# A four-layer graph network kernel: the add of beta moved from VectorE to GpSimd in the node tail, and two VectorE steps taken ahead of the scaling by gamma

## The reference, cut to what matters

```
h = relu(layernorm(x)); x = x + GAT(h)          # attention layer, two convolutions
h = relu(layernorm(x)); x = x + LightGCN(h)     # three hops of weighted sums over edges
h = relu(layernorm(x)); x = x + L2(h)           # messages and node updates
h = relu(layernorm(x)); x = x + GCN(h)          # three layers with weights conv_w
```

```
h2 = relu(layernorm(x))
update = relu(h2 @ Wu1a + bu1) @ Wu2 + bu2
x3 = x + layernorm(h2 + update) * gamma + beta
h3 = relu(layernorm(x3))
x0 = relu(h3 @ fc1 + fc1_b), then three products by conv weights with relu, then out = x3 + (...) @ fc2 + fc2_b
```

## Time and profile before

| | |
|---|---|
| median of 3 runs | 6715.88 us (6671.08 to 6734.13) |
| profiled execution, span from first to last instruction | 6034.3 us |
| the phase, 2381 to 3549 us of the span | 1168 us |
| VectorE busy in the phase | 1036.25 us |
| ScalarE busy | 773.95 us |
| PE busy | 841.98 us |
| GpSimd busy | 593.38 us |

### The profile page before, as it was taken

The page is one execution under the profiler, slowest core; times in us unless marked ns, Lnnn a source line. Parts: engine busy times, 40 slices in busy tenths (PEclk is TensorE's granted clock), DMA queues, the critical chain, the costliest instruction groups (busy, mean ns, idle before and its releaser), DMA issues. The chain is left out here.

```text
span 6034.3 us, 73632 instructions
## 1 busy us (share of the span) xinstructions
PE 3347.4 (55%) x17186; PEld 2352.5 (39%) x17363; DVE 4133.5 (68%) x14902; ACT 2890.5 (48%) x6936; POOL 3733.6 (62%) x3700
## 2 busy tenths in 40 slices
PE   0534777737330000777777758888688854454443
PEld 0423554627320000444444436666466644343322
DVE  7359999639491995998989967777377755454332
ACT  0954777313100222666666647777477743232110
POOL 0664776767675576645536546665577627676776
PEclk9767999767665555899999989999899976566666
DMA  2223665637321664434435445554244447564333
GB/s 67 80 93 119 199 200 189 191 91 192 84 51 43 163 186 124 121 109 110 116 100 121 110 128 186 189 188 158 84 151 150 141 143 246 175 200 145 119 123 100
DMA packets 512359, 827.25 MB, mean 137 GB/s; under 512 B 108999, under 2 KB 193843, under 8 KB 510796
## 3 DMA queue, kind: packets, MB, share of 16 engines
q1 hardware_dynamic: 396011, 629.55, 32.2%
q0 software_dynamic: 115936, 193.21, 14.3%
HBM read 382.25 MB, written 452.03 MB: 138 GB/s over the span
## 5 line engine op out<-in xcount | busy, mean ns | idle before, releaser
L3074 POOL DMA_INDIRECT gcn_ring<-GT,gcn_index x588 | 586.6, 998 | 199.1 <-issue 170.1
L3175 DVE SCALAR_TENSOR_TENSOR gcn_acc<-gcn_acc,cont,gcn_ring 128x128 f32<-128x128 f32 x588 | 203.6, 346 | 562.5 <-DMA gcn_ring<-GT,gcn_index 561.4
L1602 POOL DMA_INDIRECT light_ring<-C,light_s_u x392 | 390.5, 996 | 285.9 <-DVE light_acc L1645 178.7
L482 POOL DMA_INDIRECT J<-packed,sort_place x392 | 423.7, 1081 | 155.2 <-issue 120.5
L3257 PE MATMUL gcn_psA<-ident,gcn_h 128*128 128x128 f32 x588 | 154.9, 415 | 598.5 <-DVE gcn_h L3178 598.0
L3224 ACT ACTIVATE gcn_hT<-gcn_psA 128x512 f32<-128x512 f32 x147 | 87.8, 597 | 698.0 <-PE gcn_psA L3257 697.5
L3257 PEld LDWEIGHTS gcn_psA<-ident,gcn_h 128*128 128x128 f32 x588 | 100.1, 207 | 636.9 <-DVE gcn_h L3178 636.9
L1447 ACT ACTIVATE tail_h<-tail_x,tail_nmr,tail_std 128x128 f32<-128x128 f32 x784 | 320.8, 484 | 9.2 <-DVE tail_nmr L1377 9.2
L2321 POOL DMA_INDIRECT out<-source_x,source_own_u x196 | 193.7, 988 | 208.8 <-DVE source_x L2407 163.1
L473 POOL DMA_INDIRECT got_s<-TAB,src_u x196 | 202.1, 1031 | 123.7 <-issue 63.0
L1496 PE MATMUL tail_psT<-ident,tail_h 128*128 128x128 f32 x784 | 128.9, 289 | 266.3 <-ACT tail_h L1447 266.3
(11 more groups left out here) (637 smaller groups left out, 12801.6 us busy)
## 6 DMA issues: line engine op xcount, KB each, us to landing
T<-front_t SPq DMA_DIRECT2D x196, 272.0 KB, 2.1
C<-light_acc SPq DMA_DIRECT2D x147, 256.0 KB, 2.1
source_c<-C SPq DMA_DIRECT2D x147, 256.0 KB, 4.9
GT<-source_r SPq DMA_DIRECT2D x147, 256.0 KB, 2.1
gcn_own<-GT SPq DMA_DIRECT2D x147, 256.0 KB, 3.5
RC<-gcn_own SPq DMA_DIRECT2D x147, 256.0 KB, 3.6
RG<-gat_rows SPq DMA_DIRECT2D x98, 264.0 KB, 3.9
front_x<-in_x SPq DMA_DIRECT2D x98, 256.0 KB, 3.7
```

The costliest lines, as they stand in the source:

```text
L482: nc.gpsimd.indirect_dma_start(out=table, out_offset=bass.IndirectOffsetOnAxis(ap=index[:, c:c + 1], axis=0), in_=rows[:, c, :], in_offset ...
L1602: nc.gpsimd.indirect_dma_start(out=ring[:, n % RING, j, :], out_offset=None, in_=tables[h], in_offset=bass.IndirectOffsetOnAxis(ap=index[: ...
L3074: nc.gpsimd.indirect_dma_start(out=ring[:, n % RING, j, :], out_offset=None, in_=net.GT[i], in_offset=bass.IndirectOffsetOnAxis(ap=index[: ...
L3175: nc.vector.scalar_tensor_tensor(out=acc[:, n % 2, j, :], in0=before, scalar=net.cont[:, c:c + 1], in1=ring[:, n % RING, j, :], op0=ALU.mu ...
```

## The change

`Tail.pool_step` is new: for group m GpSimd waits until ScalarE has made h2 of m (which has read x) and adds beta to x in place. VectorE's beta step is gone. `shift_rows(upto)` calls it for all groups up to `upto` that were not done yet. The gather loop is regrouped by tail step: after the gathers of a step come the beta adds up to group step - 4; before the hop's end those up to the last step with sums minus 2, after the fix is placed one more. On VectorE, g1T and y now stand ahead of gamma.

```diff
+    def pool_step(self, pool, m):
+        if 0 <= m < NODE_GROUPS:
+            x2 = self.X[:, m % self.XR, :, :]
+            pool.wait_ge(self.h2_made, m + 1)
+            self.nc.gpsimd.tensor_tensor(x2, x2, slots(self.net.w["beta"]), ALU.add).then_inc(self.xb_made, 1)
...
-        m = n - 3
-        if inside(m):
-            x2, yn = self.X[:, m % self.XR, :, :], self.yn[:, m % 2, :, :]
-            v.wait_ge(self.h2_made, m + 1)
-            nc.vector.tensor_tensor(x2, x2, slots(w["beta"]), ALU.add).then_inc(self.xb_made, 1)
-            v.wait_ge(self.yn_made, m + 1)
-            nc.vector.tensor_tensor(yn, yn, slots(w["gamma"]), ALU.mult).then_inc(self.gy_made, 1)
         m = n - 5
...
+        m = n - 2
+        if inside(m):
+            v.wait_ge(self.upd_done, m + 1)
+            after(v, self.yn_made, m, 3)
+            nc.vector.tensor_tensor(self.rows(self.y, 3, m), ps["Y"][:, :], self.rows(self.h2, self.HR, m), ALU.add).then_inc(self.y_made, 1)
         m = n - 3
         if inside(m):
+            yn = self.yn[:, m % 2, :, :]
+            v.wait_ge(self.yn_made, m + 1)
+            nc.vector.tensor_tensor(yn, yn, slots(w["gamma"]), ALU.mult).then_inc(self.gy_made, 1)
             v.wait_ge(self.xb_made, m + 1)
             v.wait_ge(self.gy_made, m + 1)
...
                 for h in range(HOPS):
                     index = s_u if h else r_u
-                    for g in range(NG):
-                        n = h * NG + g
...
+                    for step in range(h * HOP_STEPS, h * HOP_STEPS + SUM_STEPS):
+                        for n in sums_of(step):
+                            if n >= RING:
+                                pool.wait_ge(chain, (n - RING + 1) * S)
...
+                        shift_rows(step - 4)
+                    shift_rows(h * HOP_STEPS + SUM_STEPS - 3)
...
                     pool.wait_ge(placed, 16 * h + 16)
+                    shift_rows(h * HOP_STEPS + HOP_STEPS - 4)
```

More of the change, by code:

```diff
@@ L1414, in vector_step @@
             nc.vector.tensor_tensor(self.rows(self.x3, self.X3R, m), self.rows(self.yn, 2, m), self.rows(self.X, self.XR, m), ALU.add).then_inc(self.x3_made, 1)
-        m = n - 2
-        if inside(m):
-            v.wait_ge(self.upd_done, m + 1)
-            after(v, self.yn_made, m, 3)
-            nc.vector.tensor_tensor(self.rows(self.y, 3, m), ps["Y"][:, :], self.rows(self.h2, self.HR, m), ALU.add).then_inc(self.y_made, 1)
         m = n - 3
@@ L1593, in _, with shift_rows @@
                 pool.wait_ge(copied, 3)
+                shifted = [0]
+                def shift_rows(upto):
+                    for m in range(shifted[0], upto + 1):
+                        tail.pool_step(pool, m)
+                    shifted[0] = max(shifted[0], upto + 1)
                 for h in range(HOPS):
                     index = s_u if h else r_u
-                    for g in range(NG):
-                        n = h * NG + g
-                        if n >= RING:
-                            pool.wait_ge(chain, (n - RING + 1) * S)
-                        for j in range(S):
-                            c = g * S + j
-                            nc.gpsimd.indirect_dma_start(
-                                out=ring[:, n % RING, j, :], out_offset=None, in_=tables[h],
-                                in_offset=bass.IndirectOffsetOnAxis(ap=index[:, c:c + 1], axis=0)).then_inc(arrived[n % RING], 16)
+                    for step in range(h * HOP_STEPS, h * HOP_STEPS + SUM_STEPS):
+                        for n in sums_of(step):
+                            if n >= RING:
+                                pool.wait_ge(chain, (n - RING + 1) * S)
+                            for j in range(S):
+                                c = n % NG * S + j
+                                nc.gpsimd.indirect_dma_start(
+                                    out=ring[:, n % RING, j, :], out_offset=None, in_=tables[h],
+                                    in_offset=bass.IndirectOffsetOnAxis(ap=index[:, c:c + 1], axis=0)).then_inc(arrived[n % RING], 16)
+                        shift_rows(step - 4)
+                    shift_rows(h * HOP_STEPS + SUM_STEPS - 3)
                     for k in range(AR):
```

## The result

The changed kernel takes 6776.43 us (median of 20 launches, 6707.53 to 6814.28), the kernel before in the same comparison 6715.44 (20 launches, 6671.08 to 6773.53). The ratio is **1.0079 [1.0054, 1.0103]**: slower by about 53 us, where 19 us less were forecast. (The ratio leaves out one launch of the changed kernel that was over 1.5% above its fastest; between the two medians lie 61 us.) The time lies outside the range of 6635 to 6760, and on the other side of no change.

What follows compares the result with a forecast made beforehand. VectorE's work was taken to bound two-group steps, a loop VectorE, ScalarE, VectorE the one-group steps; -59 - 20 + 38 + 8 + 14 = -19 us took 6715.9 to 6697, range 6635 to 6760.

Steps and rivals of the forecast that it cites:

- The base: Profiled span of 6034 us goes to 6015; what lies around it stays, so the median of 6715.9 becomes 6697.
- A: Beta's add leaves VectorE: 98 instructions at 0.60 us each, -59 us, all on VectorE's path.
- B: g1T and y stand before the wait for yn: one-group steps gain 0.4 us more over 49 steps, -20 us.
- Can ScalarE and PE follow?: Check of the loop through ScalarE and PE: one-group steps would outrun it, but their mean with two-group steps stays about 11.
- floor of 10.4: Loop through ScalarE and PE in steps without sums: cannot go under 10.87 - 0.46 = 10.4 us.
- The second rival: Loop through PE and ScalarE binds: one-group steps cannot shrink below 10.87 us; +5 us, 6721; chance 17%.
- C: GpSimd's add stops VectorE instructions with two SBUF inputs, mostly in two-group steps: +38 us, bounds 0 and 127.
- D: Start of the phase: the first add stands behind 28 gathers, so the first x3 must wait: +8 us.
- E: Hop starts: GpSimd has no lead, so for some 12 steps in each of three hops adds fall anywhere: +14 us.
- The third: Rival: every add stops VectorE in the sums, gamma or x3 for 1.3 us; +56 us, 6772; chance 12%.
- Two-group steps of 12.2: Sign that the forecast is right: two-group steps last 12.2 us between `tail_nmr`.
- one-group steps of 9.9: Sign that the forecast is right: one-group steps last 9.9 us between `tail_nmr`.

Runs made afterwards that it cites:

- e1: The kernel before, unchanged, executed once more for a second profile: 6782.43 us, span 6780.7.
- e3: Kernel before with only VectorE's order changed (g1T and y ahead of gamma), beta still added by VectorE: ratio 1.0059.
- e17: Changed kernel with six gathers issued behind each addition of beta, and each addition also waiting for g2T of its step: ratio 0.9783.
- e8: Kernel before with the gathers' lead over the sums limited to 2 groups instead of 8: ratio 0.9873.
- e9: Kernel before with VectorE's new order, beta still added by VectorE, and a gather lead of 2 groups: ratio 0.9938.
- e16: Changed kernel with six gathers issued behind each addition of beta, instead of eight and four in turn: ratio 0.9852.
- e12: Kernel before, lead kept at 8 groups, GpSimd waiting after each group of four gathers until they have landed: ratio 0.9839.
- e10: Kernel before, beta added by VectorE, order g1T, gamma, y, x3, statistics of y, statistics of x3, gather lead 2: ratio 0.9873.
- e11: Kernel before with beta's addition given to GpSimd, VectorE's old order, and a gather lead of five groups: ratio 1.0019.
- e14: Changed kernel, GpSimd waiting for each group of four gathers to land, and its addition also waiting for g2T of its step: ratio 1.0112.

## Why the prediction was wrong, point by point

- **The base.** "What lies around the span is untouched" failed: nothing lies around it. The profile was of an execution in which hardly a stall occurred, with the same rows of gathers in it: VectorE's gaps of over 2 us sum to 7 us in it and to 110 in e1. I had a difference of 682 us before me and gave it a name instead of asking what was different.
- **A, beta leaves VectorE, -59: right in size.** An undisturbed two-group step has 12.20 with the new order alone (e3) and 11.59 when beta is GpSimd's and meets nothing (e17).
- **B, g1T and y ahead, -20: the step that failed on its own sign.** The wait for yn vanished and the wait for C1 came, 43.1 us where about 48 were forecast. Measured alone, B is +40 us (e3; 44 from e8 to e9, on two chips). Two things were left out. I priced an instruction at 0.60 wherever it stands, and the order puts three that need each other side by side: 0.30 a step of VectorE's time, which shows in the two-group steps (+0.31). And "Can ScalarE and PE follow? ... it costs nothing by itself" failed: I checked the loop with TensorE at its full clock alone. Where that clock was at the lower level, one-group steps took 13 to 16 us (17 of 49 in e9, 3 in e8). The undisturbed ones fell to 10.18, by 0.70 where 0.40 was forecast and below the floor of 10.4, so the -19 that undisturbed steps alone would give agrees with the -20 by luck. The second rival named the right engines with the wrong mechanism: its floor of 10.87 does not hold.
- **C, the shared access, +38: mechanism right.** The multiply-adds went up to 1.97 us, not 1.37, and 22.4 us were lengthened in all; the second order adds to that, since a late g2T makes `conv2`, x3T and h3 late (C1 ends 3.5 behind `tail_nmr` in the one-group step and g1T waits 0.78). e17 to e16, 0.7%, or 55 us of the phase with 13 of them stalls, is the price with all that follows from it when 37 us are lengthened; what it is in the changed kernel wasn't measured. The place decides: 22, 37, 81 and 110 us for the same 98 additions.
- **D, the first addition, +8: not seen.** The first addition ended at 2714.2, and the first x3 began at 2729.89, because y had waited 22.51 us until 2728.49. In e1 y waits 18.84 there as well. A stall during the first 28 gathers covers the addition.
- **E, hop starts, +14:** not to be told apart from C; the 22.4 hold both.
- **The missing term, stalls, +41,** is the largest, and the step that the forecast lacks altogether. The change makes the gathers wait behind an addition that waits for h2, and so ties each row of eight to a place in the step where PE's products are needed next. In the changed kernel the seventh of eight begins most often 0.7 or 11 us behind `tail_nmr`, just ahead of g2T, the output addition and g1T. In the kernel before, eight gathers in a row begin behind a sum, so that the seventh begins 7.9 us behind it (e1), beside statistics and sums, which read nothing of PE. I moved the queue past a wait and costed only what stands in it.
- **The rivals.** The third (slower, 6772) came within 5 us of the time for a wrong reason: it needed 0.72 us lost per addition, and 0.23 were lengthened. "Two-group steps of 12.2" came as 12.74, "one-group steps of 9.9" as 10.97 at best.

## What to carry to other kernels

Take a second profile, or compare the span with the timed launches, before trusting a profile that is 10% off: steady stalls may be missing from it. When a step is to become shorter, check the loop over TensorE at both of its clock levels. When a wait is put into a queue that issues transfers, ask not only who waits for the added work, but when the transfers now go out and what runs beside them. Offload element-wise work to GpSimd only where it falls beside instructions with an operand in PSUM, and keep an independent instruction between two that depend on each other.

## What the hardware showed that I had not expected

- **Gathers in a row go with late signals from PE.** From about the seventh indirect transfer that GpSimd issued without a break, VectorE and ScalarE stood before PE's products although those are recorded as done 4.5 and 6.1 us earlier: 3 to 5 us behind rows of eight, 16 and 17 us behind rows of 32. PE's semaphore updates came that late, and those of VectorE and ScalarE in the changed kernel were on time. A pause ended it (e12). Six gathers with an addition between did not, where nothing was waited for (11.5 us in e16). What the chip does there isn't settled: ends of PE's instructions are modelled, so PE itself may have been late, and in one execution (6034 us) rows of 60 and more did nothing. Taking turns with another kind of transfer wasn't tried.
- **TensorE's granted clock sets the price of a new order elsewhere.** After idle times of about 5 us TensorE ran at 0.50 for the next products, a pair in 1.92 us instead of 1.02, and one-group steps of 10.2 us became 13 to 16 (e9).
- **The result of one VectorE instruction costs the next 0.13 to 0.17 us more** when that next one needs it (0.73 and 0.77 in place of 0.60 from start to start). In two-group steps this shows as 12.20 us against 11.96 (e9, e10), in undisturbed one-group steps not at all (10.18 against 10.28).
- **A VectorE instruction with both inputs in SBUF stands for the whole of GpSimd's addition**, 1.27 us and 0.56 behind it (e11), and one that reads PSUM hardly notices it: 0.5 us in all for 98 additions (e14).
